# Expert pairs on TensorE in longer rows: sixteen transposes, both up halves, four down products, over one ring of six PSUM banks

## The reference

```python
shared = jax.nn.silu(g_s) * y_s @ w_shared_down
scores = jax.nn.sigmoid(x_flat @ w_gate)
_, topk_idx = jax.lax.top_k(scores, TOPK)               # TOPK = 6
...
x_disp = jnp.zeros((E, CAP, C), x.dtype).at[flat_e, pos].set(x_flat[token_ids], mode='drop')   # 64 x 256 x 512
up = jnp.einsum('ecd,edh->ech', x_disp, w_up)
g_r, v_r = jnp.split(up, 2, axis=-1)
h_r = jax.nn.silu(g_r) * v_r
out_r = jnp.einsum('ech,ehd->ecd', h_r, w_down)
y_ts = out_r[flat_e, pos_c]
...
routed = (y_ts.reshape(N, TOPK, C) * w[:, :, None]).sum(axis=1)
return (shared + routed).reshape(B, T, C)
```

## Time and profile before

| | us |
|---|---|
| median of three executions | 1126.71 (1125.02 to 1128.56) |
| span of the profiled execution | 1137.7 |
| PE busy | 1041.9 (92%) |
| DVE busy | 681.7 (60%) |
| POOL busy | 485.5 (43%) |
| ACT busy | 322.6 (28%) |

### The profile page before, as it was taken

The page is one execution under the profiler, slowest core; times in us unless marked ns, Lnnn a source line. Parts: engine busy times, 40 slices in busy tenths (PEclk is TensorE's granted clock), DMA queues, the critical chain, the costliest instruction groups (busy, mean ns, idle before and its releaser), DMA issues.

```text
span 1137.7 us, 16279 instructions
## 1 busy us (share of the span) xinstructions
PE 1041.9 (92%) x6109; PEld 570.0 (50%) x6110; DVE 681.7 (60%) x1290; ACT 322.6 (28%) x446; POOL 485.5 (43%) x468
## 2 busy tenths in 40 slices
PE   7988889999999999999999987789999999998586
PEld 6975544554454554545544622347555555554232
DVE  3331463778878787787788755763444444443366
ACT  3420023224133232232241321432433333333121
POOL 1100013625655665647657485054344454445100
PEclk9997999999999999999999996899999999999799
DMA  8872079579580580661603141436879999983898
GB/s 310 298 312 93 1 268 375 192 289 336 184 327 30 187 316 20 243 241 65 217 1 113 77 156 73 182 133 256 301 286 392 374 366 341 376 290 140 330 409 321
DMA packets 93786, 262.30 MB, mean 231 GB/s; under 512 B 10623, under 2 KB 10751, under 8 KB 92944
## 3 DMA queue, kind: packets, MB, share of 16 engines
q1 hardware_dynamic: 43920, 146.18, 35.1%
q10 hardware_dynamic: 31872, 63.97, 15.2%
q0 software_dynamic: 17920, 51.15, 11.5%
HBM read 129.91 MB, written 139.72 MB: 237 GB/s over the span
## 4 chain that ended last, share of the span: by engine, by line
PE 76%; DMA 7%; DVE 6%; issue 4%; ACT 3%; POOL 3%; another core or an unknown queue 1%; SPq 0%; POOLq 0%; ACTq 0%; DVEq 0%
PE banks L1178 18%; PE banks L1186 10%; PE banks L1687 10%; PE banks L1279 6%; PE banks L1319 6%; PE banks L1698 6%; DMA e_eo<-y_d 6%; PE banks L1673 6%; PE banks L1337 4%; DVE t_nmx L992 3%; PE banks L1200 2%; ACT t_probs L791 1%; PE banks L1172 1%; POOL t_psum L703 1%; PE banks L391 1%
## 5 line engine op out<-in xcount | busy, mean ns | idle before, releaser
L1526 POOL DMA_INDIRECT y_d<-e_eo,e_ids x128 | 124.5, 972 | 148.4 <-DVE e_eo L1615 117.2
L992 DVE TENSOR_REDUCE t_nmx<-banks 128x4 f32<-128x2048 f32 x64 | 146.4, 2288 | 55.0 <-PE banks L1279 54.9
L703 POOL TENSOR_TENSOR t_psum<-t_psum,t_probs 128x512 f32<-128x512 f32 x112 | 140.8, 1289 | 63.0 <-ACT t_probs L791 61.5
L791 ACT ACTIVATE t_probs<-banks 128x2048 f32<-128x2048 f32 x56 | 105.1, 1878 | 149.6 <-PE banks L1322 139.0
L715 POOL DMA_INDIRECT xs_d<-r_norm,r_xaddr x96 | 96.5, 1005 | 52.1 <-DVE r_xaddr L1125 26.5
L1279 PE MATMUL banks<-b_key,b_qry 32*128 32x512 f32 x512 | 77.1, 673 | 25.4 <-DVE t_nmx L992 19.0
L675 POOL TENSOR_TENSOR f_rstd<-f_veps,mhalf 128x2 f32<-128x2 f32 x24 | 16.9, 706 | 189.1 <-DVE f_veps L893 189.0
L1319 PE MATMUL banks<-b_qry,b_key 32*128 32x512 f32 x512 | 73.9, 647 | 16.0 <-ACT t_probs L791 7.3
L703 POOL TENSOR_TENSOR t_psum<-t_probs,t_probs 128x512 f32<-128x512 f32 x56 | 72.0, 1319 | 16.3 <-ACT t_probs L791 14.3
L1673 PE MATMUL banks<-ident,e_xg 128*128 128x128 f32 x512 | 70.4, 280 | 1.6 <-DMA e_xg<-xs_d 0.9
L1673 PEld LDWEIGHTS banks<-ident,e_xg 128*128 128x128 f32 x512 | 54.8, 141 | 26.2 <-issue 24.3
(11 more groups left out here) (217 smaller groups left out, 1653.8 us busy)
## 6 DMA issues: line engine op xcount, KB each, us to landing
xs_d<-zero ACTq DMA_DIRECT2D x32, 1056.0 KB, 9.9
e_xg<-xs_d SPq DMA_DIRECT2D x32, 1056.0 KB
y_d<-zero ACTq DMA_DIRECT2D x24, 1024.0 KB
e_xg<-y_d SPq DMA_DIRECT2D x16, 768.0 KB, 15.1
e_eo<-y_d SPq DMA_DIRECT2D x16, 768.0 KB, 14.5
wo<-in_wud SPq DMA_DIRECT2D x8, 768.0 KB
wupT<-in_wud SPq DMA_DIRECT2D x8, 768.0 KB
wdnT<-in_wud SPq DMA_DIRECT2D x8, 768.0 KB
```

Source lines behind the costliest of these rows:

```text
L703: ins = g_.tensor_tensor(psum0[:, q, :], first[:, q, :], probs[s % NP][:, q, :], ALU.add)
L791: A(probs[s % NP][:, :, :], quad[:, :, :], ACT.Exp, scale=SCALE1).then_inc(W["exp_ok"], 1)
L992: V.tensor_reduce(nmx[g][:, m, :], quad[:, :, :], axis=AX.X, op=ALU.max, negate=True).then_inc(W["mx_ok"], 1)
L1526: g_.indirect_dma_start(out=y_d, out_offset=bass.IndirectOffsetOnAxis(ap=ids[:, HC * p + n:HC * p + n + 1], axis=0), in_=eo[u][:, n, :], i ...
```

## The change

The order on TensorE, ScalarE and VectorE within an iteration is another one. Iteration p is now `transpose(p + 2, 0)`, `transpose(p + 2, 1)`, `up(p, 0)`, `up(p, 1)`, `down(p - 1, 0)`, `down(p - 1, 1)`. A small function `downs_after` says which pairs' down products stand at the end of an iteration: that of p - 1, in iteration 30 those of pairs 29 and 30, in iteration 31 that of 31. The six banks of the transposes and the down products become one ring: each fill takes the next bank, and waits for the copy of the fill six before it (`ring_turns`, `open_ring`). The five waits on semaphores of the part before stand now behind the transposes of pair 0, which wait for its `exp_ok` in their place. The code of SP and GpSimd is the same.

```diff
+def ring_turns(banks, tiles, halves):
+
+    fills = []
+    turns = lambda p: [("turn", p, e, t) for e in range(tiles // halves) for t in range(halves)]
+    downs = lambda p: [("down", p, t, e) for t in range(halves) for e in range(tiles // halves)]
+    for p in (0, 1):
+        fills += turns(p)
+    for p in range(PAIRS):
+        fills += turns(p + 2) if p + 2 < PAIRS else []
+        fills += [f for q in downs_after(p) for f in downs(q)]
+    copied = lambda kind, p, a, b: ("xA_ok", "xB_ok")[b] if kind == "turn" else ("oA_ok", "oB_ok")[b]
+    slot_of = {f: i % banks for i, f in enumerate(fills)}
+    before = {f: (copied(*fills[i - banks]), halves * fills[i - banks][1] + fills[i - banks][2] + 1)
+              for i, f in enumerate(fills) if i >= banks}
+    return slot_of, before
+
+
+def downs_after(p):
+
+    if p == PAIRS - 1:
+        return [p]
+    return [p - 1, p] if p == PAIRS - 2 else [p - 1][:p]
...
-    pT, pU = v["work"][0:HT], [v["work"][HT], v["pV"]]
+    pU = [v["work"][HT], v["pV"]]
     pD = [v["quad"][:, k, :] for k in range(HC)]
+    ring = pD + v["work"][0:HT]
+    slot_of, before = ring_turns(len(ring), HC, HT)
...
-            A(xT[p % 3][:, e, :, 0:P], pT[0][:, :].rearrange("p (k s) -> p k s", k=KC), ACT.Copy).then_inc(xA_ok, 1)
+            A(xT[p % 3][:, e, :, 0:P], ring[slot_of["turn", p, e, 0]][:, :].rearrange("p (k s) -> p k s", k=KC), ACT.Copy).then_inc(xA_ok, 1)
...
             gated(p)
-            for t in range(HT):
-                if p + 2 < PAIRS:
-                    turned(p + 2, t)
-                if p:
-                    evicted(p - 1, t)
+            for q in downs_after(p):
+                for t in range(HT):
+                    evicted(q, t)
...
-                if t == 0:
-                    hidden(p)
             if p + 2 < PAIRS:
+                for e in range(2):
+                    turned(p + 2, e)
                 identify(p + 2)
+            hidden(p)
+            for q in downs_after(p):
+                for t in range(HT):
+                    evicted(q, t)
             if 1 <= p <= NB // 2:
                 for b in range(2 * p - 2, 2 * p):
                     shared_gate(b)
-        for t in range(HT):
-            evicted(PAIRS - 1, t)
...
+        copied = dict(xA_ok=xA_ok, xB_ok=xB_ok, oA_ok=oA_ok, oB_ok=oB_ok)
+
+        def open_ring(*fill):
+            if fill in before:
+                s, n = before[fill]
+                pe.wait_ge(copied[s], n)
+            return ring[slot_of[fill]]
...
-                since(pe, (xA_ok, xB_ok)[t], 2 * p + e)
+                dst = open_ring("turn", p, e, t)
                 for k in range(KC):
-                    last = tr(pT[t][:, k * P:(k + 1) * P], xg[u][:, HT * e + t, k * P:(k + 1) * P], ident[:, :])
+                    last = tr(dst[:, k * P:(k + 1) * P], xg[u][:, HT * e + t, k * P:(k + 1) * P], ident[:, :])
...
-            since(pe, oA_ok, HT * (p - 1) + t + 1)
-            since(pe, oB_ok, HT * (p - 1) + t + 1)
+            dst = [open_ring("down", p, t, e) for e in range(2)]
...
-        pe.wait_ge(W["x4T_ok"], T * NB)
-        pe.wait_ge(W["sums_ok"], T * NB)
-        pe.wait_ge(W["eg_ok"], NB - 1 + T)
-        pe.wait_ge(W["pos_ok"], NB - 1 + T)
-        pe.wait_ge(W["raw_ok"], NB)
+        pe.wait_ge(W["exp_ok"], 8 * NB)
         for p in range(2):
             for e in range(2):
                 transpose(p, e)
+                if p == 0 and e == 1:
+                    pe.wait_ge(W["x4T_ok"], T * NB)
+                    pe.wait_ge(W["sums_ok"], T * NB)
+                    pe.wait_ge(W["eg_ok"], NB - 1 + T)
+                    pe.wait_ge(W["pos_ok"], NB - 1 + T)
+                    pe.wait_ge(W["raw_ok"], NB)
         pe.wait_ge(W["kept_ok"], 2 * NB)
         for p in range(PAIRS):
-            for t in range(HT):
-                up(p, t)
-                if p + 2 < PAIRS:
-                    transpose(p + 2, t)
-                if p:
-                    down(p - 1, t)
-        for t in range(HT):
-            down(PAIRS - 1, t)
+            if p + 2 < PAIRS:
+                for e in range(2):
+                    transpose(p + 2, e)
+            for j in range(2):
+                up(p, j)
+            for q in downs_after(p):
+                for t in range(HT):
+                    down(q, t)
```

More of the change, by code:

```diff
@@ L1545, in evicted @@
             act.wait_ge(dn_mm, HT * p + t + 1)
-            A(eo[p % OB][:, t, :], pD[2 * t][:, :], ACT.Copy).then_inc(oA_ok, 1)
+            A(eo[p % OB][:, t, :], ring[slot_of["down", p, t, 0]][:, :], ACT.Copy).then_inc(oA_ok, 1)
         act.wait_ge(W["y_zero"], 16 * (NB * S * TOPK // (P * HC)))
@@ L1590, in turned @@
             since(dve, up_mm, p - 2)
-            V.tensor_copy(xT[p % 3][:, e, :, P:2 * P], pT[1][:, :].rearrange("p (k s) -> p k s", k=KC)).then_inc(xB_ok, 1)
+            V.tensor_copy(xT[p % 3][:, e, :, P:2 * P], ring[slot_of["turn", p, e, 1]][:, :].rearrange("p (k s) -> p k s", k=KC)).then_inc(xB_ok, 1)
         def identify(p):
@@ L1614, in evicted @@
             dve.wait_ge(dn_mm, HT * p + t + 1)
-            V.tensor_copy(eo[p % OB][:, HT + t, :], pD[2 * t + 1][:, :]).then_inc(oB_ok, 1)
+            V.tensor_copy(eo[p % OB][:, HT + t, :], ring[slot_of["down", p, t, 1]][:, :]).then_inc(oB_ok, 1)
         for u in range(2):
@@ L1694, in down @@
                 pe.wait_ge(h_ok, p + 1)
-            since(pe, oA_ok, HT * (p - 1) + t + 1)
-            since(pe, oB_ok, HT * (p - 1) + t + 1)
+            dst = [open_ring("down", p, t, e) for e in range(2)]
             for e in range(2):
-                last = mm(pD[2 * t + e][:, :], hT[p % 2][HE * e:HE * (e + 1), t * P:(t + 1) * P], wd[u][HE * e:HE * (e + 1), :],
+                last = mm(dst[e][:, :], hT[p % 2][HE * e:HE * (e + 1), t * P:(t + 1) * P], wd[u][HE * e:HE * (e + 1), :],
                           start=True, stop=True)
             last.then_inc(dn_mm, 1)
-        pe.wait_ge(W["x4T_ok"], T * NB)
-        pe.wait_ge(W["sums_ok"], T * NB)
-        pe.wait_ge(W["eg_ok"], NB - 1 + T)
-        pe.wait_ge(W["pos_ok"], NB - 1 + T)
-        pe.wait_ge(W["raw_ok"], NB)
+        pe.wait_ge(W["exp_ok"], 8 * NB)
         for p in range(2):
```

## The result

| | before | changed |
|---|---|---|
| median of the runs beside each other (3 and 4) | 1126.71 us | 1114.14 us |
| ratio, with its 95% interval | | 0.9897 [0.9872, 0.9923] |
| profiled execution, its span | 1137.7 | 1114.5 |
| from the start of the last sixteen products of the shared expert's up half to the last scatter | 269.35 | 255.53 |

The change makes the kernel 1.0% faster; the medians lie 12.6 us apart. A fourth run of the kernel before, with 1245.04 us in a slower state of the chip, is left out. The forecast was 1109.0 with a range from 1104.5 to 1117, so the time is inside, 5 us above the forecast.

What follows compares the result with a forecast made beforehand. TensorE was taken as the bound, at 7.92 us a pair with no idle time. Savings of 14.2 + 0.3 + 1.7 + 1.4 = 17.6 us off 1126.7 gave 1109.1, said as 1109, range 1104.5 to 1117.

Steps and rivals of the forecast that it cites:

- Seams: TensorE's changes of kind, six a pair before and three now: 0.49 us saved in each of 29 iterations, 14.2 us.
- The start: Iteration 0 on TensorE, 5.5 us instead of 5.8: 0.3 us saved, between 1 lost and 1 won.
- Waits for copies: Ring fills waiting for the copy six fills before: cost 0, nearest margin 0.9 us at the third group of transposes.
- The weights: TensorE's wait for pair 6's weights falls from 2.74 to 1.0 us, 1.7 saved; the other loads 0.
- rival A: Transfers become the bound at 354 GB/s; pairs from about 8 to 25 stay at 7.92, losing 8.8 us: 1118; chance 0.10.
- The end: Start of iteration 30 to GpSimd's last scatter, 19.7 us with twelve scatters in a row, instead of 21.1: 1.4 saved.
- B: Half the seams on TensorE stay, belonging to new banks or group waits; half of 14.2 us lost: 1116; chance 0.12.
- C: TensorE's clock falls with sixteen transposes in a row, making the kernel slower: 72 us more, 1181; chance 0.02.
- D: A copy stands in the way: the ring's nearest wait costs 0.5 us a pair, all 14.2 lost: 1123; chance 0.04.

Runs made afterwards that it cites:

- the first occasion: First of three occasions of follow-up runs, each on another chip; the unedited kernel before had a median of 1139.04 us there.
- after_acc_late: Changed kernel with the four accumulator loads issued behind the last load of weights; 1129.15 us, ratio 0.9903 to the kernel before.
- by_twos: Changed kernel with the transposes of two pairs in a row and the down products of two pairs, every second iteration; 1112.34 us, ratio 0.9862 to before.
- by_twos_acc_late: by_twos with the four accumulator loads issued behind the last load of weights; 1105.98 us, ratio 0.9819 to the kernel before.
- end_apart: Changed kernel with pair 30's down products kept in the last iteration, 31; 1115.92 us in one run.
- the two kernels of half the order: Changed kernel with the two experts' transposes apart, 1115.57 us; changed kernel with ups and downs alternating by halves again, 1120.4 us; one run each.
- after_again: Changed kernel, unedited, timed again beside the kernel before on another chip; 1129.98 us, ratio 0.9913.
- own_banks: Changed kernel's order with the banks of before, two for transposes and four for down products; 1147.8 us, ratio 1.0076 to the kernel before.
- after_extra: Changed kernel with 0.27 MB more loaded per iteration from pair 4 on, into a tile nobody reads; 1127.26 us in one run.

## Why the prediction was right, and where its sum was off

*Seams, 14.2 forecast.* Right, in the mechanism and in the size. From the start of iteration 1 to that of iteration 30 it took 232.54 us (29 pairs of 7.92 and the wait), and now 218.60 (29 pairs of 7.42 and the waits). The seams are 29 x 0.50 = 14.5.

*The start, 0.3 forecast.* 0.65, inside the bounds given. TensorE began iteration 0 9.61 us after the start of the last sixteen shared products, where it was 9.93, and the iteration is 0.33 shorter.

*Waits for copies, 0 forecast.* Right everywhere but on the first occasion, where the margin of 0.9 us was used up in ten to twelve pairs. VectorE's copy of a down product begins 1.2 us after its start, as assumed:

```profile
882.02 0.69 DVE L1640 COPY e_eo<-banks 128x512 f32<-128x512 f32 x1 [0.65 <-PE banks L1726]
```

*The weights, 1.7 and 0 forecast: mis-sized.* They came to 0.5 lost, not 1.7 won. The wait before iteration 6 went from 2.74 to 1.45, and so gave 1.3. But the chain before the waits shows what I had put at 0:

```profile
823.98 8.64 DMA wdnT<-in_wud
...
905.12 16.82 DMA wdnT<-in_wud
...
949.92 18.19 DMA wo<-in_wud
```

The first is the load of the earlier trace rows, 0.6 longer than it was. The other two are the loads behind the third and fourth accumulator load. I had argued with the mean rate of long stretches, "with little to spare", and the mean was indeed reached: 393 and 388 GB/s. What a mean can't show is one large extra load ahead of the one that is waited for, with iterations that come 0.5 us sooner each; with the accumulator loads moved (after_acc_late) the waits are 0. This is a part of rival A, about a fifth of its 8.8 us, and by_twos, at 7.245 us a pair, shows how it grows. For the full rival, the Trainium skill (DMA: Bandwidth & Descriptors, Where 436 GB/s comes from) gives about 358 GB/s as a core's half of a stack's 716. This kernel runs on one core, and the trace does not show that limit, with 393 and 388 over 63 us each.

*The end, 1.4 forecast: mis-sized.* It took 21.85 us from the start of iteration 30 to the last scatter, against 21.08: 0.8 lost. Two things were off in it. The hand-over from an eviction to GpSimd takes 0.86 (883.57 in the scatters after 882.02 + 0.69 of the row above; it is the same for 1011.64), where my estimate was 0.1: 0.76 us. And GpSimd pauses between its 113th and its 114th scatter, 3.05 us from one to the other where it is otherwise 1.28. The pause was there before too, hidden in idle time that followed. Now pair 29's tiles are ready while GpSimd is still 1.4 us from the end of pair 28's, so the last run begins with pair 28 and has the pause in it: 15 x 1.28 + 1.77 = 21.0 us from 1011.64 to 1032.61. By the terms of the forecast, 3.6 + 1.87 + 0.86 + 14.1 = 20.4, and 1.4 of the pause makes 21.8. by_twos and by_twos_acc_late have no such pause, and they take 20.45 and 20.48. end_apart confirms that nothing on TensorE counts in it.

*The rivals.* B fell with the two kernels of half the order. C, a falling clock, did not come: the granted clock was 1.00 from 790 to 1020 us, with sixteen transposes in a row, and in the stretch of pairs of by_twos with 32. Where it fell in the pairs of other kernels, for 3.4 us, it was behind a wait for weights. The rule of the Trainium skill (TensorE: Matmul & The Clock Gate, Part 4: PE-mode transpose) that would have made C likely finds no support in any run here. D appeared on the first occasion alone, at about a third of its price (0.16 us on average in after_again) and in 12 of the 29 pairs. Without the ring a wait of its kind costs 0.56 in every pair (own_banks).

*The sum.* 14.5 + 0.65 - 0.5 - 0.8 = 13.8 against 17.6. Of the 3.8 that are missing the weights are 2.2 and the end is 2.2; the seams and the start gave 0.65 more. The mechanism of the main term was right. The two small terms, forecast as 3.1 us won together, were 1.3 us lost. The time still came inside the range because the range had 8 us of room above the forecast, put there for seams that might stay and for a part of rival A. The span of the changed kernel, forecast as 1120.1, was 1114.5: the 11.0 us between the span and the median of before did not carry over, and 8.5 us of it lie ahead of the experts. They cancel in the forecast of the median.

## What to carry to other kernels

In this kernel a change from one shape of product to another has a price on TensorE even when nothing waits, 0.14 to 0.21 us; it can be read from the starts of single instructions at the seams and added up by kind, and the sum held to hundredths. A tighter order needs buffers to match: the same order with banks of its own for each kind took 7.98 us a pair, against 7.92 in the order it came from. And where one engine gets faster, look at the queue of the next one instruction by instruction, not at its mean rate: an occasional large load ahead of an urgent one, or a pause that idle time had covered, takes back a part of the gain, and by_twos earned the larger part of its gain over the changed kernel only when the loads were moved out of the way (0.9885 to 0.9862, then to 0.9819).

## What the hardware showed that I had not expected

- A wait of TensorE is at times followed by 3.4 us at half the clock (0.52 and 0.51 in the rows of after_again and after_extra), which costs 1.7 us more. It came behind waits of 2.02, 2.29, 3.69 and 3.70 us, and not behind those of 2.12, 2.74, 2.77, 2.96 and 3.81 in kernels of this case, so the length of the wait alone does not decide it.
- GpSimd pauses ahead of the 114th scatter by 1.77 us more than its usual 0.30 (the row of 1014.69 above), and ahead of the 18th by 1.3, with nothing that it waits for in the profile. Both stand at the same instructions in every kernel but the two by_twos, which have no such pause; there the scatter just ahead of these two places does not follow a wait, as it does in the others. Why is open.
- On one occasion the other engines saw TensorE's results late, by about 1 us in the middle of the stage and by several at its end, in kernels with long rows of one kind and not in the one with short rows. It shows as a wait where the order has little slack. The granted clock was 1.00 when it set in, and why it comes is open.
